# ScalarE instead of SyncE issues the transfers that bring the turned squares of attention back

## The chip, the cores and the metric

The kernel runs on one core of one Trainium2 chip. The metric is device time in microseconds (us), from a single launch; lower is better. The engines of the core are TensorE (PE in the profile), VectorE (DVE), ScalarE (ACT), GpSimd (POOL) and SyncE (SP); each runs its own instructions in the order in which they are written, and a wait in front of an instruction holds back all that is behind it on that engine. DMA transfers are issued by SP, ACT or POOL and moved by 16 DMA engines.

## The reference

```python
x = hidden_states                       # (2, 1024, 512) float32
xn = layernorm(x)
q = dequant_matmul(xn, qw_q, scales_q)  # 32 heads of 128; weights (512, 4096), 4-bit values as int32
k = dequant_matmul(xn, qw_k, scales_k)  # 8 key heads of 128
v = dequant_matmul(xn, qw_v, scales_v)
q, k = apply_rope(q), apply_rope(k)
scores = q @ k.T / sqrt(128)            # causal mask, 1024 x 1024 for each of 2 x 32 heads
ctx = softmax(scores) @ v
attn = dequant_matmul(ctx, qw_o, scales_o)
ffn = xn @ W_base.T + b_base + lora_of_top_2_of_8_experts(xn)
out = x + attn + ffn                    # (2, 1024, 512)
```

A dequantised weight is (value - 8) times a scale that holds for 128 rows of the input dimension.

## The kernel before

All products are made in float32 precision from pairs: every operand is split into a high part (rounded to the format that TensorE takes at full rate) and a low part (the remainder), and three matmuls high x high, low x high and high x low make one product. ScalarE makes most high parts with a copy, POOL and VectorE make the low parts by subtraction.

The work is cut into 16 units (2 batches of 8 key heads; `UNITS`), each with 4 query heads. Below, "unit 9, head 1" is counted from zero; "the second head of a unit" is head 1. Batch `PARKED` is normalised first, parked in HBM, and brought back between unit 7 and unit 8: POOL issues the reload of `xnT_high` and `xnT_low` (line 774), SP that of Y.

A query head goes like this. TensorE makes eight rows of tiles of scores (`scores`, line 1451); row i has i + 1 tiles of 128 x 128. VectorE takes the row's maximum (line 1187), ScalarE the exponential (line 945, `exps`). The second product wants the probabilities transposed. For query rows 0 to 3, and for the part right of the first four key tiles in rows 4 to 7, TensorE transposes them (`turn`, line 1462); ScalarE makes `PT_high` from it (`high`, line 871), VectorE `PT_low` (line 1100). The remaining square, query rows 4 to 7 against keys 0 to 511, is transposed without TensorE. VectorE transposes each of its four row blocks in 32 x 32 pieces (`turn_squares`, line 1194). SP sends each block to HBM (`move_out`, line 594, tile `squares`, 256 KB). When all four have landed, four transfers of 256 KB bring them back in the arrangement that finishes the transpose (`move_in`, line 608, tile `moved`), one for each group of 32 partitions. ScalarE makes `moved_high` from `moved` (`moved_tile_high`, line 871), POOL makes `moved_low` (`moved_tile_low`, line 797), in four tiles j = 0 to 3, with two buffers. `values` (line 1317, output `O_ps`) multiplies turned and moved tiles with V: for c = 0 (query rows 0 to 3) the turned tiles 0 to 3; for c = 1 the order of tiles is 0, 4, 5, 1, 6, 2, 7, 3, of which 0 to 3 are the moved ones. So moved tile 0 is the first thing that c = 1 needs.

Between these steps TensorE projects the queries and keys of the heads to come (`project`) and multiplies finished contexts with the output weights (`output`). A projected half of Q or K passes through VectorE (`terms`, lines 1167 to 1172), POOL (`rope_add`, line 804), ScalarE (`rope_high`, line 871, `Q_high` or `K_high`) and POOL again (`rope_low`, line 812, `Q_low`). POOL also dequantises and splits the weights (lines 738, 739, 758, 759), which SP loads (`load_scales`, line 552; `load_raw`, line 560). A buffer's load waits until POOL has read what stood in it.

The order on TensorE is a list `STEPS`, written by hand from patterns for each head. The order on every other engine is derived from it. `begins` gives each step a planned begin with rough lengths, and `behind(STEPS, us, kinds)` gives for each step of a kind the place in the list at which it is due, `us` microseconds after the planned end of that step. Each engine walks through the list and at each place emits what is due there, in the fixed order of the statements in its loop. For SP: row sums out, squares out (due 3.0 after `scores`), squares in (due 7.0 after the head's last row of scores), row sums in, scales, raw weights, outputs. For ScalarE: high parts of turned tiles (due -0.3), reads of the low-rank product, exponentials (2.6 after `scores`), moved tiles, V, rope copies (4.0 after `project`), contexts. `Seen` leaves out a wait that an earlier one of the same engine already implies.

In the written order, SP's four transfers back stand behind the last transfer out and the load of row sums (`R_sb`), and in the second head of even units behind one pair of weight loads as well; other weight loads that are due soon stand behind them.

Of the kernel before, what the change touches and what calls it, by code (L numbers as in the profile page):

```python
# [178 lines left out]
def behind(steps, us, *kinds):  # L179

    at = begins(steps)
    due, n = [[] for _ in at], 0
    for k, s in enumerate(steps):
        if s[0] in kinds:
            while n < len(steps) and at[n] < at[k] + length(s) + us:
                n += 1
            due[n].append(s)
    return due
# [65 lines left out]
def build_program(nc, x, scales_q, scales_k, scales_v, scales_o, qw_q, qw_k, qw_v, qw_o,  # L254
# [5 lines left out]
    STEPS = tensor_order()  # L260
# [26 lines left out]
    with ctx:  # L287
# [24 lines left out]
        moved = sb("moved", [P, 16, MOVED, 32])  # L312
# [175 lines left out]
        def head_of(u, h):  # L488
            return u * REP + h
# [40 lines left out]
        def _(sp):  # L530
# [63 lines left out]
                sp.dma_start(squares[n % 2][i - 4].rearrange("p (b n) -> p b n", b=4),  # L594
                             row_squares(i).rearrange("p (b n) -> p b n", b=4)).then_inc(moved_out[i - 4], 16)

            def move_in(u, h):
                n = head_of(u, h)
                for i in range(4):
                    if seen.new(moved_out[i], 16 * (n + 1)):  # L600
                        sp.wait_ge(moved_out[i], 16 * (n + 1))
                if n:

                    if seen.new(moved_done, 4 * n):
                        sp.wait_ge(moved_done, 4 * n)
                back = squares[n % 2].rearrange("r (a k) (b n) -> b k (r a) n", a=4, b=4)
                for b in range(4):
                    sp.dma_start(moved[32 * b:32 * (b + 1), :, :, :].rearrange("p t j q -> p t (j q)"),  # L608
                                 back[b]).then_inc(moved_in[n % 2], 16)

            def load_x(b, c):
                if b != PARKED:
                    if seen.new(y_put[c], 16):
# [61 lines left out]
            scales_due, raw_due = weights_due(STEPS, -7.0), weights_due(STEPS, -6.0)  # L675
            sums = behind(STEPS, 3.8, "scores")
            divided, sums_there = behind(STEPS, 0.2, "values"), behind(STEPS, 9.8, "scores")
            squares_out, squares_in = behind(STEPS, 3.0, "scores"), behind(STEPS, 7.0, "scores")
            outputs = behind(STEPS, 1.0, "output")
            turned_now, linear = behind(STEPS, 0.8, "turn_x"), behind(STEPS, 0.6, "lora_b")  # L680
            for n in range(len(STEPS) + 1):
                for _, u, h, i in sums[n]:
                    if i % 4 == 3:
                        store_sums(u, h, i // 4)
                for _, u, h, i in squares_out[n]:
                    if i >= 4:
                        move_out(u, h, i)
                for _, u, h, i in squares_in[n]:
                    if i == 7:
                        move_in(u, h)  # L690

                for _, u, h, i in sums_there[n]:
                    if (u, h, i) == (0, 0, 3):
                        load_sums(u, h, 0)
                for _, u, h, c, j in divided[n]:
                    if j == 3 and (u, h, c) != (UNITS - 1, REP - 1, 1):
                        load_sums(*((u, h, 1) if c == 0 else (*divmod(head_of(u, h) + 1, REP), 0)))
                for u, w in scales_due[n]:
                    load_scales(u, w)
                for u, w in raw_due[n]:  # L700
                    load_raw(u, w)
                for _, u, p, t in outputs[n]:
                    if u + 1 == UNITS and p == 1:
                        store_tile(u // NKV, t)
                    elif u % NKV == NKV - 1 and p == 1 and t % 4 == 3:
                        store_y(u // NKV, t // 4)
                        load_parked_y(t // 4)
                for _, b, t in turned_now[n]:
                    if b == PARKED and t % 4 == 3:
                        load_rows(t // 4)  # L710
                        park_xn(t // 4)
                for _, b, t in linear[n]:
                    if b == PARKED and t % 4 == 3:
                        park_y(t // 4)
                        load_x(STARTED[1], t // 4)
                        if t == 3:
                            load_tables()
# [149 lines left out]
        def _(act):  # L867
# [5 lines left out]
            def linear_weights():  # L873
                for name, src in (("ar", ar_t), ("b", b_t), ("base", w_base_t)):
                    n = {"ar": KT * AR, "b": HID, "base": KT * HID}[name]
                    dst = lin_raw[:, RAW[name]:RAW[name] + n]
                    if name != "b":
                        src, dst = src.rearrange("(k p) n -> p k n", p=P), dst.rearrange("p (k n) -> p k n", k=KT)
                    act.dma_start(dst, src).then_inc(lin_loaded[name], 16)
                act.dma_start(bias[:, :], b_base.to_broadcast([P, HID])).then_inc(lin_loaded["bias"], 16)  # L880
# [29 lines left out]
            def high(*step):  # L910
# [6 lines left out]
                dst, _, src = split_of(step)  # L917
                copy(dst, src).then_inc(pt_high, 1)

            moved_order = itertools.count()  # L920

            def moved_tile_high(u, h, j):
# [52 lines left out]
            moved_due = [behind(STEPS, us, "scores") for us in (15.5, 18.1)]  # L975
            multiplied = behind(STEPS, -0.2, "values")
            divided, low_rank = behind(STEPS, 1.2, "values"), behind(STEPS, -0.6, "lora_a")
            linear_weights()
            linear_weight_high("ar")
            root(PARKED, 0, 2)  # L980
            for n in range(len(STEPS) + 1):
                for s in turned_now[n]:
                    high(*s)
                    if s == ("turn_x", PARKED, 1):
                        root(PARKED, 2, 4)
                        linear_weight_high("b")
                    if s == ("turn_x", PARKED, 3):
                        root(PARKED, 4, 6)
                    if s == ("turn_x", PARKED, 5):
                        root(PARKED, 6, 8)  # L990
                    if s[:2] == ("turn_x", PARKED) and 2 <= s[2] < 2 + KT:
                        linear_weight_high("base", s[2] - 2)
                    if s == ("turn_hidden", PARKED, 1):
                        root(STARTED[1], 0, 4)
                        root(STARTED[1], 4, 8)
                for _, b, t in low_rank[n]:
                    lora_read(b, t)
                    if t == NT - 1:
                        route_exps(b)
                for _, u, h, i in scored[n]:  # L1000
                    exps(u, h, i)
                for j, due in enumerate(moved_due):
                    for _, u, h, i in due[n]:
                        if i == 7:
                            moved_tile_high(u, h, j)
                for _, u, h, c, j in multiplied[n]:
                    if c and j < 2:
                        moved_tile_high(u, h, j + 2)
                for _, u, t in projected[n]:
                    value_high(u, t)  # L1010
                for _, u, w, c in rotated[n]:
                    rope_high(u, w, c)
                for _, u, h, c, j in divided[n]:
                    if j == 3:
                        context_high(u, h, c)
# [566 lines left out]
```

## Time and profile before

| | us |
|---|---|
| median of 2 runs | 2031.91 (2031.89 to 2031.93) |
| the profiled execution, its own time | 2028.99 |
| its span, first to last instruction | 2027.2 |
| TensorE busy | 1987.2 (98%) |
| VectorE busy | 1488.9 (73%) |
| ScalarE busy | 983.2 (48%) |
| POOL busy | 1527.7 (75%) |
| mean granted TensorE clock | 0.996 |
| mean rate of the DMA engines | 138 GB/s |

Busy times are sums of the durations of an engine's instructions; issuing DMAs and waiting are not counted as busy. In the profile, an entry such as `Q_high<-rope` names output and input tile. "idle before <-releaser" is the time an engine stood still ahead of an instruction and what ended it. SPq and ACTq are the sequencers of SP and ACT, where the issue of a transfer is recorded; its duration there is the time that the issue takes on that engine and not the transfer's.

### The profile page before, as it was taken

Reading aid. Unit: us, or ns where it says so; the run is one execution under the profiler, and the core shown is the slowest. Engines: PE = TensorE matmul, PEld = TensorE weight load, DVE = VectorE, ACT = ScalarE, POOL = GpSimd, SP = SyncE. Lnnn points to the kernel's source line nnn. Section 1 sums busy time; section 2 is a strip of 40 time slices with the busy share of each in tenths; the row PEclk is TensorE's granted clock in tenths of the full one; section 3 lists DMA queues with packets and bytes.
Section 4 is the critical chain, followed back from the end, with each engine's and each line's share of the span. In section 5 each row is a group of like instructions: output and inputs, shape, how many; then the busy total and the mean of one; then the engine's idle time right before and its main releaser. Section 6 shows DMA issues by size and latency. Waiting matters only on the chain.

```text
span 2027.2 us, 31353 instructions
## 1 busy us (share of the span) xinstructions
PE 1987.2 (98%) x10666; PEld 1693.1 (84%) x10668; DVE 1488.9 (73%) x3059; ACT 983.2 (48%) x2202; POOL 1527.7 (75%) x1376
## 2 busy tenths in 40 slices
PE   8999999999999999999989999999999999999998
PEld 6888888888888888888878888888888888888887
DVE  6757777777777777677766777777777777767775
ACT  3145554454544455455534545445554545545453
POOL 2657789677878779786886869867787877968683
PEclk9999999999999999999999999999999999999999
DMA  6326465454635546453583645454464545535454
GB/s 227 137 73 154 110 153 136 127 135 120 167 110 136 130 135 158 110 151 105 151 223 110 208 126 157 116 153 128 118 156 115 146 115 155 158 94 141 126 147 112
DMA packets 302422, 280.17 MB, mean 138 GB/s; under 512 B 34584, under 2 KB 215736, under 8 KB 301752
## 3 DMA queue, kind: packets, MB, share of 16 engines
q1 hardware_dynamic: 298808, 272.13, 50.3%
q0 software_dynamic: 2112, 4.19, 0.7%
q8 instruction: 85, 1.39, 0.3%
q10 hardware_dynamic: 1344, 1.85, 0.3%
q14 instruction: 73, 0.60, 0.1%
HBM read 200.25 MB, written 77.94 MB: 137 GB/s over the span
## 4 chain that ended last, share of the span: by engine, by line
PE 74%; DMA 8%; DVE 7%; POOL 7%; issue 2%; SPq 1%; ACT 1%; DVEq 0%; POOLq 0%; ACTq 0%
PE ring L1317 37%; PE O_ps L1317 16%; PE ring L1451 16%; PE turned L1462 5%; DMA moved<-squares 5%; POOL moved_low L797 3%; DMA squares<-probs 2%; DVE probs L1194 2%; DVE ctx_f L1224 1%; POOL scl L739 1%; DVE probs L1187 1%; SPq L608 1%; POOL W_low L759 1%; POOL ctx_low L821 1%; DVE rope L1171 1%
## 5 line engine op out<-in xcount | busy, mean ns | idle before, releaser
L945 ACT ACTIVATE probs<-probs,negmax 128x128 f32<-128x128 f32 (+7 forms) x512 | 396.2, 774 | 153.5 <-DVE negmax L1187 153.3
L1187 DVE CUSTOM_DVE_ANT_0 probs<-ring,mask_row 128x128 f32<-128x128 f32 (+7 forms) x512 | 373.6, 745 | 41.1 <-PE ring L1451 40.8
L797 POOL TENSOR_TENSOR moved_low<-moved,moved_high 128x512 fp32r<-128x512 f32 x256 | 328.7, 1293 | 76.0 <-ACT moved_high L871 74.6
L1100 DVE TENSOR_TENSOR PT_low<-turned,PT_high 128x512 fp32r<-128x512 f32 (+3 forms) x515 | 245.2, 489 | 178.4 <-ACT PT_high L871 97.2
L871 ACT ACTIVATE PT_high<-turned 128x512 fp32r<-128x512 f32 (+3 forms) x515 | 213.6, 433 | 324.1 <-PE turned L1462 301.5
L821 POOL TENSOR_TENSOR ctx_low<-ctx_f,ctx_high 128x512 fp32r<-128x512 f32 (+1 forms) x131 | 165.9, 1267 | 178.2 <-ACT ctx_high L871 178.2
L804 POOL TENSOR_TENSOR rope<-rope 128x512 f32<-128x512 f32 x160 | 206.9, 1293 | 80.9 <-DVE rope L1172 80.9
L1317 PE MATMUL ring<-xnT_high,W_high 128*128 128x512 f32 x640 | 254.9, 398 | 0.0
L1317 PE MATMUL ring<-xnT_high,W_low 128*128 128x512 f32 x640 | 250.6, 392 | 0.0
L1317 PE MATMUL ring<-xnT_low,W_high 128*128 128x512 f32 x640 | 249.5, 390 | 0.0
L1451 PE MATMUL ring<-K_high,Q_high 128*128 128x512 f32 (+3 forms) x768 | 233.9, 359 | 0.9 <-POOL Q_low L812 0.6
L1451 PE MATMUL ring<-K_high,Q_low 128*128 128x512 f32 (+3 forms) x768 | 225.4, 348 | 0.0
L1451 PE MATMUL ring<-K_low,Q_high 128*128 128x512 f32 (+3 forms) x768 | 225.1, 347 | 0.0
L1234 DVE TENSOR_TENSOR Y<-ring,Y 128x512 f32<-128x512 f32 x256 | 175.7, 688 | 62.7 <-PE ring L1317 60.5
L1462 PE MATMUL turned<-ident,probs 128*128 128x128 f32 x1280 | 219.3, 275 | 0.0
L759 POOL TENSOR_TENSOR W_low<-scl,W_high 128x512 fp32r<-128x512 f32 x160 | 206.9, 1293 | 13.3
L739 POOL TENSOR_TENSOR scl<-raw,scl 128x512 f32<-128x512 f32 x160 | 206.7, 1292 | 13.4
L1167 DVE TENSOR_TENSOR rope<-ring,cos_sb 128x512 f32<-128x512 f32 x160 | 110.7, 692 | 143.2 <-PE ring L1317 137.9
L871 ACT ACTIVATE moved_high<-moved 128x512 fp32r<-128x512 f32 x256 | 159.5, 626 | 112.0 <-DMA moved<-squares 59.9
L871 ACT ACTIVATE Q_high<-rope 128x512 fp32r<-128x512 f32 x128 | 80.9, 632 | 267.3 <-POOL rope L804 267.3
L1317 PE MATMUL ring<-W_high,ctx_high 128*128 128x512 f32 x512 | 206.9, 404 | 1.4 <-POOL ctx_low L821 1.4
L1317 PE MATMUL ring<-W_high,ctx_low 128*128 128x512 f32 x512 | 201.2, 393 | 0.0
(124 smaller groups left out, 4680.6 us busy)
## 6 DMA issues: line engine op xcount, KB each, us to landing
squares<-probs SPq DMA_DIRECT2D x256, 256.0 KB, 2.9
moved<-squares SPq DMA_DIRECT2D x256, 256.0 KB, 4.7
R_sb<-row_sums SPq DMA_DIRECT2D x128, 256.0 KB, 3.7
scl<-packed_q SPq DMA_DIRECT2D x64, 256.0 KB, 5.0
raw<-in_qw_q SPq DMA_DIRECT2D x64, 256.0 KB, 5.0
scl<-in_scales_o SPq DMA_DIRECT2D x64, 256.0 KB, 4.7
raw<-in_qw_o SPq DMA_DIRECT2D x64, 256.0 KB, 2.9
scl<-packed_k SPq DMA_DIRECT2D x16, 256.0 KB, 4.2
```

Source lines behind the costliest of these rows:

```text
L739: nc.gpsimd.tensor_tensor(out=scl[:, n % 2, :], in0=as_float, in1=scl[:, n % 2, :], op=ALU.mult).then_inc(scaled, 1)
L759: nc.gpsimd.tensor_tensor(out=W_low[:, slot, :], in0=scl[:, n % 2, :], in1=W_high[:, slot, :].bitcast(f32), op=ALU.subtract).then_inc(w_do ...
L797: nc.gpsimd.tensor_tensor(out=low, in0=moved[:, :, j, :], in1=high.bitcast(f32), op=ALU.subtract).then_inc(moved_done, 1)
L804: nc.gpsimd.tensor_tensor(out=rope_a[:, n % 2, :], in0=rope_a[:, n % 2, :], in1=rope_b, op=ALU.add).then_inc(rope_sum, 1)
L821: nc.gpsimd.tensor_tensor(out=ctx_low[:, at, cols], in0=ctx_f[:, cols], in1=ctx_high[:, at, cols].bitcast(f32), op=ALU.subtract).then_inc( ...
L871: return nc.scalar.activation(dst, src, ACT.Copy)
L945: nc.scalar.activation(probs[:, at], probs[:, at], ACT.Exp, bias=negmax[:, i:i + 1], scale=-1.0, accum_out=sums[:, i:i + 1]).then_inc(exp_ ...
L1100: nc.vector.tensor_tensor(out=dst, in0=src, in1=high.bitcast(f32), op=ALU.subtract).then_inc(pt_low, 1)
L1187: nc.vector.tensor_tensor_reduce(row, ps, hidden_keys, -1.0, -MASKED, ALU.add, ALU.min, negmax[:, i:i + 1]).then_inc(negmax_ready, 1)
L1317: mm = nc.tensor.matmul(dst, lhs, rhs, start=start and n == 0, stop=stop and n == len(terms) - 1)
L1451: mm = nc.tensor.matmul(ps[:, lo:hi], lhs[:, tile], moving, start=first, stop=last)
L1462: mm = nc.tensor.transpose(turned_place(step)[:, q * P:(q + 1) * P], probs[:, at:at + P], ident[:, :])
```

## The change

`move_in` is taken out of SP's program and put into ScalarE's, with the same waits (all four blocks landed in HBM; the moved tiles of the head before read by POOL), the same four transfers and the same semaphores. It keeps its due time, 7.0 us after the last row of scores. In ScalarE's loop it stands behind the exponentials and ahead of the moved tiles.

```diff
@@ SP @@
-            def move_in(u, h):
-                n = head_of(u, h)
-                for i in range(4):
-                    if seen.new(moved_out[i], 16 * (n + 1)):
-                        sp.wait_ge(moved_out[i], 16 * (n + 1))
-                if n:
-
-                    if seen.new(moved_done, 4 * n):
-                        sp.wait_ge(moved_done, 4 * n)
-                back = squares[n % 2].rearrange("r (a k) (b n) -> b k (r a) n", a=4, b=4)
-                for b in range(4):
-                    sp.dma_start(moved[32 * b:32 * (b + 1), :, :, :].rearrange("p t j q -> p t (j q)"),
-                                 back[b]).then_inc(moved_in[n % 2], 16)
...
-            squares_out, squares_in = behind(STEPS, 3.0, "scores"), behind(STEPS, 7.0, "scores")
+            squares_out = behind(STEPS, 3.0, "scores")
...
-                for _, u, h, i in squares_in[n]:
-                    if i == 7:
-                        move_in(u, h)
@@ ScalarE @@
+            def move_in(u, h):
+                n = head_of(u, h)
+                for i in range(4):
+                    if seen.new(moved_out[i], 16 * (n + 1)):
+                        act.wait_ge(moved_out[i], 16 * (n + 1))
+                if n:
+
+                    if seen.new(moved_done, 4 * n):
+                        act.wait_ge(moved_done, 4 * n)
+                back = squares[n % 2].rearrange("r (a k) (b n) -> b k (r a) n", a=4, b=4)
+                for b in range(4):
+                    act.dma_start(moved[32 * b:32 * (b + 1), :, :, :].rearrange("p t j q -> p t (j q)"),
+                                 back[b]).then_inc(moved_in[n % 2], 16)
...
+            squares_in = behind(STEPS, 7.0, "scores")
...
                 for _, u, h, i in scored[n]:
                     exps(u, h, i)
+                for _, u, h, i in squares_in[n]:
+                    if i == 7:
+                        move_in(u, h)
                 for j, due in enumerate(moved_due):
```

## Rows read from the trace of the kernel before

**Rows 1.** Waits of TensorE: engine, line, waited for, us in total, times, longest.
```profile
PE O_ps L1317 <- POOL moved_low L797: 9.1, 8, 6.4
```

**Rows 2.** Waits of SP's sequencer, the same columns.
```profile
SPq L601 <- DMA squares<-probs: 160.1, 64, 4.7
```

**Rows 3.** Chain of waits from 1010 to 1045 us: start, us, what.
```profile
1016.69 3.81 DMA squares<-probs
...
1020.65 0.32 SPq L608
...
1022.60 12.06 DMA moved<-squares
```

**Rows 4.** Timeline of SP, unit 9, head 1: start, us, instruction, count.
```profile
1238.04 1.91 SPq L608 DMA_DIRECT2D moved<-squares  x4
...
1240.86 0.43 SPq L560 DMA_DIRECT2D raw<-in_qw_q  x1
```

**Rows 5.** Timeline of ScalarE, the same head.
```profile
1236.18 0.98 ACT L871 ACTIVATE PT_high<-turned 128x512 fp32r<-128x512 f32 x2 [2.55 <-PE turned L1462]
1237.89 0.63 ACT L871 ACTIVATE Q_high<-rope 128x512 fp32r<-128x512 f32 x1 [0.73 <-POOL rope L804]
1239.50 0.38 ACT L871 ACTIVATE PT_high<-turned 128x256 fp32r<-128x256 f32 x1 [0.98 <-PE turned L1462]
```

**Rows 6.** Timeline of POOL, the same head.
```profile
1239.89 1.29 POOL L812 TENSOR_TENSOR Q_low<-rope,Q_high 128x512 fp32r<-128x512 f32 x1
...
1245.13 1.29 POOL L812 TENSOR_TENSOR Q_low<-rope,Q_high 128x512 fp32r<-128x512 f32 x1 [0.74 <-ACT Q_high L871]
1246.38 2.55 POOL L797 TENSOR_TENSOR moved_low<-moved,moved_high 128x512 fp32r<-128x512 f32 x2
```

**Rows 7.** Timeline of TensorE, the same head.
```profile
1243.39 0.28 PE L1317 MATMUL O_ps<-PT_high,V_high 128*128 128x256 f32 x1
...
1248.35 0.39 PE L1317 MATMUL O_ps<-moved_high,V_high 128*128 128x512 f32 x1
```

**Rows 8.** Timeline of SP, unit 1, head 2.
```profile
308.43 2.90 SPq L608 DMA_DIRECT2D moved<-squares  x4
```

**Rows 9.** Timeline of POOL, the same head.
```profile
309.90 1.30 POOL L812 TENSOR_TENSOR Q_low<-rope,Q_high 128x512 fp32r<-128x512 f32 x1
...
316.38 2.71 POOL L797 TENSOR_TENSOR moved_low<-moved,moved_high 128x512 fp32r<-128x512 f32 x2
```

**Rows 10.** Timeline of TensorE, the same head.
```profile
318.35 0.39 PE L1317 MATMUL O_ps<-moved_high,V_high 128*128 128x512 f32 x1
```

**Rows 11.** The tile moved: its issues, with duration in ns min/median/max.
```profile
L608 SPq DMA_DIRECT2D moved<-squares x256: 303/487/1820, 135.5 to 2002.8; - x128
```

**Rows 12.** Timeline of ScalarE's sequencer at the start, two of its four issues.
```profile
0.75 0.46 ACTq L879 DMA_DIRECT2D probs<-in_ar_t  x1
...
2.27 0.85 ACTq L880 DMA_DIRECT2D R_sb<-in_b_base  x1
```

**Rows 13.** DMA queues from 1026 to 1029 us: packets, MB, share of 16 engines.
```profile
q0 software_dynamic: 376, 0.77, 84.3%
q1 hardware_dynamic: 368, 0.18, 43.5%
```

**Rows 14.** Chain of waits of the whole span, one of its longest pieces.
```profile
282.01 7.23 DMA moved<-squares
```

**Rows 15.** Timeline of ScalarE, unit 2, head 1.
```profile
413.18 0.63 ACT L871 ACTIVATE moved_high<-moved 128x512 fp32r<-128x512 f32 x1 [2.94 <-DMA moved<-squares]
```

**Rows 16.** Timeline of TensorE, the same head.
```profile
415.24 0.49 PE L1317 MATMUL O_ps<-moved_high,V_high 128*128 128x512 f32 x1
```

**Rows 17.** Busy time by stretch: PE, PEld, DVE, ACT, POOL, PEclk, DMA share, GB/s.
```profile
1036.00:1040.00 4.00, 3.30 (x9) 2.62 (x9) 2.06 (x7) 2.98 (x9) 3.45 (x4) 0.50 1.24 382
1040.00:1044.00 4.00, 4.00 (x20) 3.50 (x18) 2.46 (x9) 2.57 (x7) 3.92 (x5) 0.76 0.56 156
```

**Rows 18.** Page, part 3, a DMA queue: packets, MB, share of 16 engines.
```profile
q10 hardware_dynamic: 1344, 1.85, 0.3%
```

## The prediction

> **What bounds the kernel now.** I read the waits of TensorE first, because the page gives it 98% of the span. The reader is to see how little of its idle time hangs on the moved tiles: 9.1 us in 8 waits, and 6.4 us of that is one wait [rows 1]. Even a perfect change cannot return more than that and the clock time behind it; the rest of 2027 us is TensorE at work. Next SP's own waits: 64 waits at line 601, 160.1 us, released by a DMA and not by an engine, 2.5 us each [rows 2]. So when SP comes to the moved square it is early and waits for the last square to reach HBM. The chain shows one case whole: the last square is issued at 1016.69 and lands 3.81 us later, at 1020.50, and SP issues the first transfer back at 1020.65, 0.15 us after it [rows 3]. I compared the two times in all 64 heads; the distance is 0.09 to 0.16 us in every one. **SP is never late**, so ScalarE cannot issue earlier; it issues at the same moment, or later if it is busy. Then I read ScalarE, POOL and TensorE in that stretch of a head, in a head of unit 9 [rows 4 to 7] and one of unit 1 [rows 8 to 10].
>
> **What is moved: one wait and four issues a head.** Taken off SP: the wait (2.5 us) and four issues of 0.49 us median, together 1.91 us in the unit 9 head and 2.90 us in the unit 1 head [rows 4, 8]; the longest single issue took 1.82 us [rows 11]. What SP holds behind them are the loads of the next weight's scales and raw values and later of the row sums. POOL needs those loads many microseconds later, so SP's freedom is worth nothing by itself: 0. If POOL did wait for them, the cover would be TensorE's own queue of ready work.
>
> Put on ScalarE: its position. Working out the written order gives, for the second and third heads of a unit, PT_high of turned tiles 0 and 1, then the four issues, then the first Q_high, then PT_high of tiles 2 and 3. Price of one issue on ScalarE: the trace has only its four loads at the start, the first 0.46 and the longest 0.85 us [rows 12]; SP's median for the transfers in question is 0.49 [rows 11], near the first. The same four transfers are issued, so I take SP's own durations head by head (about 1.95 us for four) and keep 4 x 0.85 = 3.4 us as the upper end, 4 x 0.30 = 1.2 us (SP's shortest) as the lower.
>
> *Turned tiles behind the issues.* In unit 9, ScalarE is free at 1237.16 (two copies from 1236.18, 0.98 us) [rows 5]. It would wait for the landing, issue from 1238.04 to 1239.95, do Q_high until 1240.63 and the next PT_high until 1241.0, where it now starts at 1239.50. TensorE takes that tile at 1243.39 [rows 7], and only VectorE's short subtraction lies between. Cover 2.4 us, so 0. If it were gone each microsecond of ScalarE would be one of TensorE.
>
> *Q_high, and POOL behind it.* This is what is late next. Q_high moves from 1237.89 to 1240.00, ends at 1240.63, and Q_low on POOL starts at 1240.70 and not at 1239.89: +0.8 us [rows 5, 6]. From that Q_low to moved_low POOL has no free time but 0.74 us [rows 6], and that is its own round trip to ScalarE for the second half, which moves along. So moved_low starts at 1247.2 and not at 1246.38; the first of the pair (half of 2.55 us, 1.27) ends at 1248.45. TensorE now reads it at 1248.35 [rows 7]. Stall: 0.1 us. In unit 1: issues 308.43 to 311.33, Q_high to 312.0, Q_low at 312.05 for 309.90, +2.15 us; moved_low, now 316.38 to 317.67, ends at 319.8; TensorE reads at 318.35 [rows 8 to 10]. Stall: 1.45 us. I did the same for every head. 20 get a stall, nearly all in the first three heads of odd units: 0.03 to 1.9 us each, together 12 us. With 1.2 us for four issues the same working gives 2 us, with 3.4 us it gives 45.
>
> *The other heads.* In the fourth heads and the first heads of even units the copy behind the issues slips by up to 4 us too, but TensorE reads the moved tile 4 to 6 us after it is ready: 0. The third heads of even units have 1.2 us and slip by nothing. In the last head nothing but turned tile 4 is behind the issues and it starts after them: 0.
>
> *The transfers.* SP's raw load now starts while the moved square is in flight, on another queue; before it stood behind it. I price the overlap by the reload between batches, where two queues were busy: 376 packets of one, 368 of the other, one for one [rows 13]. A 256 KB load beside a 1024 KB square that takes 7.2 us from its last issue to landing [rows 14] can cost up to a quarter of its flow, 1.3 us, and 0 if it falls outside. It counts only where nothing else covers it, as in the second heads of even units: there moved_high starts as the data lands (idle 2.94 us until the DMA) and TensorE reads the product at once [rows 15, 16]. About ten such heads at 0.3 us: 3 us (0 to 13). The Trainium skill says in "DMA: Bandwidth & Descriptors", section "Issuing engines are not separate DMA queues", that DMAs of all issuers run on the same 16 engines and interleave, so that another issuer saves sequencer time alone. By that rule the sum has no gain; the packets of rows 13 agree.
>
> *The change of batch.* The 6.4 us wait is the moved square of unit 7, head 2, 12.06 us in flight [rows 1, 3] beside the xnT reload; the granted clock is 0.50 from 1036 to 1040 right after TensorE stood still [rows 17], the 1.2 GHz level. ScalarE would issue at the same 1020.6; a third queue makes it a little later: +1 us (-9 to +6).
>
> **Sum.** 12 + 3 + 1 = +16 us on the profiled execution, which took 2028.99 us with a span of 2027.2. The median of the runs is 2031.91, 2.9 us above it; I add the 16 to that: **2048 us**.
>
> **Rivals.**
> 1. *All of it is hidden.* POOL's chain or TensorE's waits shift as a whole and the small stalls take each other's place: 2032, between 2028 and 2036. For it: 44 of 64 heads get no stall in the working above, and 16 of the 20 others under 1 us. Against: POOL's gapless stretch [rows 6].
> 2. *ScalarE becomes the bound, slower by over 2%.* Place: Q_high behind the four issues. Price: if an issue on ScalarE costs what the longest seen there did, 0.85 us, the POOL step above gives 45 us and not 12, and with transfers and reload 49: 2081. With SP's longest, 1.82 us, the same working stalls 55 heads for 207 us: 2243. It passes 2% (41 us in all) from about 0.8 us an issue. For it: both engines now issue at once, and the unit 1 head shows 2.90 us for four where 1.91 is usual [rows 4, 8]. Against: the 0.85 us transfer repeats one row over all partitions, the squares don't.
> 3. *A gain at the change of batch.* The square, alone on its queue, is served sooner; the 6.4 us wait goes, and so does the half clock behind it (half of 3.3 us and 0.24 of 4 us [rows 17], 2.6 us): 2032 - 9 = 2023. Against: the reload takes half of the packets in either case.
> 4. *The issuer is moved but nothing else*, since the queues are one: then rows of ScalarE's queue would be missing. The page has a queue of 1.85 MB, which is the sum of ScalarE's four loads [rows 18], so it has one of its own. I give this no chance of its own; its time would be that of rival 1.
>
> **Chances.** Forecast (4 to 38 us slower) 0.60; rival 1 0.22; rival 3 0.07; rival 2 0.11, of which 0.10 over 2%. A difference of 2% is about what a measurement of this kernel can tell from no change. The range takes in rival 1 and the forecast: 2028 to 2070. So over 2% faster 0.01, within 2% 0.89, over 2% slower 0.10.
>
> **What would show it.** ScalarE's queue has 256 issues of about 0.5 us (near 0.85: rival 2). The first starts 0.1 to 0.2 us after the last square lands. Q_high and Q_low in the unit 9 head start about 2.1 and 0.8 us later against TensorE's own work. TensorE's waits for moved_low grow from 8 to some 25 and from 9.1 to about 25 us, each under 2 us, with no half clock. SP issues raw before the fourth moved transfer. If TensorE's waits for moved_low stay at 9 us, the POOL step is wrong; if they shift to PT_low, the cover of turned tiles is.

## The result: 2109.31 us, 3.9% slower

The changed kernel takes 2109.31 us (two runs, 2105.49 and 2113.14) against 2031.91, a ratio of 1.0391 with a 95% interval of 1.0364 to 1.0418. The forecast was 2048 with a range to 2070: the sign was right, the size was not (+77 us measured, +16 forecast). The profiled execution has a span of 2111.3 us against 2027.2.

**The profile after.** First the page of the changed kernel: busy time by engine, the two hardware DMA queues (packets, MB, share of 16 engines), and the issues of the tile that was moved (KB each, median us to landing).

```profile
PE 2011.9 (95%) x10668; PEld 1700.0 (81%) x10668; DVE 1486.6 (70%) x3059; ACT 970.7 (46%) x2202; POOL 1530.2 (72%) x1376
...
q1 hardware_dynamic: 163640, 205.01, 33.1%
q10 hardware_dynamic: 136512, 68.98, 16.5%
...
moved<-squares ACTq DMA_DIRECT2D x256, 256.0 KB, 5.7
```

ScalarE's queue, q10, had 1.85 MB [rows 18] and has 68.98 now: the change does what it says. The span outside PE's busy time was 2027.2 - 1987.2 = 40.0 us and is 2111.3 - 2011.9 = 99.4: 59 of the 84 us are TensorE standing still. PE's busy time grew by 24.7 us for the same matmuls, and the mean granted clock of the execution (view of cores) fell from 0.996 to 0.986. That is at most 21 us, an estimate (0.014 x 2111 less 0.004 x 2027): in part of the time at the lower clock TensorE stands still anyway. Experiment 2 has what else makes busy time grow. The bytes to be moved are the same, but the tile takes 5.7 us to land where it took 4.7.

TensorE's waits, in the view of waits (us in total, times, longest):

```profile
PE O_ps L1318 <- POOL moved_low L780: 51.4, 30, 15.2
PE O_ps L1318 <- DVE PT_low L1101: 18.9, 21, 2.6
```

The first answers to [rows 1], 9.1 us in 8 waits: +42.3. Sorted by head, the first heads of odd units have 20.6 us of it (1.3 before), the head at the change of batch 15.2 (6.4), and the other second and third heads of odd units 10.9 (0.8). The wait for PT_low was this in the kernel before, the same view:

```profile
PE O_ps L1317 <- DVE PT_low L1100: 4.4, 6, 1.9
```

It grew by 14.5. Together 57 of the 59 us. The issues themselves and the time to landing, from the view of the tile moved:

```profile
L914 ACTq DMA_DIRECT2D moved<-squares x256: 309/510/1395, 134.5 to 2086.9; - x128
...
DMA to landing us min/median/max: 3.0/5.8/21.9
```

An issue on ScalarE costs 0.51 us where SP's cost 0.49 [rows 11]: ScalarE is hardly the dearer engine.

**The head of rows 4 to 7**, unit 9, head 1, in the changed kernel. SP, ScalarE, POOL and TensorE, one timeline each:

```profile
1291.87 0.43 SPq L552 DMA_DIRECT2D scl<-packed_q  x1
1296.53 0.38 SPq L560 DMA_DIRECT2D raw<-in_qw_q  x1
```

```profile
1292.75 0.98 ACT L854 ACTIVATE PT_high<-turned 128x512 fp32r<-128x512 f32 x2 [2.54 <-PE turned L1463]
1295.28 1.93 ACTq L914 DMA_DIRECT2D moved<-squares  x4
1297.25 0.63 ACT L854 ACTIVATE Q_high<-rope 128x512 fp32r<-128x512 f32 x1 [3.52 <-issue]
1297.79 0.54 ACT L854 ACTIVATE PT_high<-turned 128x256 fp32r<-128x256 f32 x2
```

```profile
1297.96 1.29 POOL L795 TENSOR_TENSOR Q_low<-rope,Q_high 128x512 fp32r<-128x512 f32 x1 [1.46 <-ACT Q_high L854]
...
1303.21 1.30 POOL L795 TENSOR_TENSOR Q_low<-rope,Q_high 128x512 fp32r<-128x512 f32 x1 [0.74 <-ACT Q_high L854]
1304.47 2.52 POOL L780 TENSOR_TENSOR moved_low<-moved,moved_high 128x512 fp32r<-128x512 f32 x2
```

```profile
1305.80 0.50 PE L1318 MATMUL O_ps<-moved_high,V_high 128*128 128x512 f32 x1 [0.72 <-POOL moved_low L780]
```

This is the step that the forecast described: the copies of [rows 5] wait behind 1.93 us of issues, Q_low behind Q_high, moved_low behind that, and TensorE waits 0.72 us where 0.1 us was forecast. The forecast left the issues where SP had them. They start 0.7 us later, measured from the start of the PT_high ahead of them (2.53 us behind it, 1.86 in [rows 4, 5]), because the last square lands later. In experiment 2 they start 1.0 us later in this head and the wait is 0.99 us, so the slip needs no change of the loads. In [rows 8 to 10]'s head, unit 1, head 2, the forecast was a stall of 1.45 us; TensorE's timeline there:

```profile
332.13 0.50 PE L1318 MATMUL O_ps<-moved_high,V_high 128*128 128x512 f32 x1 [1.30 <-POOL moved_low L780]
```

**What the forecast did not have** is in the first head of the same unit 9. Changed kernel, timelines of SP, then ScalarE, then TensorE:

```profile
1262.21 0.46 SPq L552 DMA_DIRECT2D scl<-packed_q  x1
1264.10 0.38 SPq L560 DMA_DIRECT2D raw<-in_qw_q  x1
```

```profile
1264.40 2.07 ACTq L914 DMA_DIRECT2D moved<-squares  x4
...
1274.84 0.63 ACT L854 ACTIVATE moved_high<-moved 128x512 fp32r<-128x512 f32 x1 [2.44 <-DMA moved<-squares]
```

```profile
1276.86 0.49 PE L1318 MATMUL O_ps<-moved_high,V_high 128*128 128x512 f32 x1 [2.08 <-POOL moved_low L780]
```

SP, free of the wait, issues the scales 2.2 us before the squares and the raw load 0.3 us before them. In the kernel before, SP did it the other way round, in the same head:

```profile
1211.50 1.91 SPq L608 DMA_DIRECT2D moved<-squares  x4
1213.45 0.49 SPq L552 DMA_DIRECT2D scl<-packed_q  x1
1213.98 0.43 SPq L560 DMA_DIRECT2D raw<-in_qw_q  x1
```

The DMA queues in the changed kernel, from 0.4 us before the first issue of the squares (1264 to 1267 us) and then from 1267 to 1270 us (packets, MB, share of 16 engines):

```profile
q1 hardware_dynamic: 403, 0.47, 84.3%
q10 hardware_dynamic: 10, 0.01, 0.6%
```

```profile
q10 hardware_dynamic: 939, 0.47, 76.4%
q1 hardware_dynamic: 349, 0.19, 30.4%
```

and in the kernel before in the 3 us from its first issue, 1211.5 to 1214.5:

```profile
q1 hardware_dynamic: 971, 0.57, 73.2%
```

In the 2.6 us from its first issue the square gets 10 packets through; before, the one queue moved 971 in 3 us, most of them the square's (819 if the window starts 0.4 us earlier, as above). It lands 10.4 us after the first issue (1274.8); before, `moved_high` started without waiting, at most 7.0 us after the first issue:

```profile
1218.46 0.62 ACT L871 ACTIVATE moved_high<-moved 128x512 fp32r<-128x512 f32 x1
```

Over the eight first heads of odd units the mean from first issue to landing went from 7.3 to 10.7 us, over the third heads of even units it stayed at 7.0. Over the third heads of odd units it went from 7.9 to 10.1, much of that at the change of batch (14.0 to 23.3); the other seven went from 7.1 to 8.2. Behind the 2.08 us wait of unit 9, head 0, TensorE's granted clock is 0.50, the 1.2 GHz level; the columns are those of [rows 17]:

```profile
1278.00:1280.00 2.00, 2.00 (x8) 1.61 (x6) 1.11 (x6) 1.03 (x4) 1.83 (x3) 0.50 0.00 0
```

**The change of batch**, unit 7, head 2. From the chain of waits, and by stretch (the columns of [rows 17]):

```profile
1060.30 21.88 DMA moved<-squares
```

```profile
1084.00:1088.00 4.00, 3.78 (x9) 3.02 (x10) 2.40 (x8) 2.51 (x8) 3.57 (x5) 0.50 0.00 0
```

The piece of [rows 3] that was 12.06 us is 21.88; TensorE stands 15.2 us where it stood 6.4, and works on at the 1.2 GHz level (0.50) behind it, as in [rows 17].

### The profile page after: what moved, and what is told of

The parts are those of the page before. It is cut to its first block, busy times and chain, and to the rows that moved or that the text cites. A ratio compares the mean times of both kernels' runs of the same rounds, so it can differ in the third digit from the quotient of the medians.

```text
span 2111.3 us, 31355 instructions
## 1 busy us (share of the span) xinstructions
PE 2011.9 (95%) x10668; PEld 1700.0 (81%) x10668; DVE 1486.6 (70%) x3059; ACT 970.7 (46%) x2202; POOL 1530.2 (72%) x1376
## 3 DMA queue, kind: packets, MB, share of 16 engines
q10 hardware_dynamic: 136512, 68.98, 16.5%
## 4 chain that ended last, share of the span: by engine, by line
PE 49%; DMA 16%; POOL 13%; DVE 10%; issue 4%; ACTq 3%; ACT 3%; SPq 1%; DVEq 0%; POOLq 0%
PE ring L1318 21%; PE O_ps L1318 13%; PE ring L1452 12%; DMA moved<-squares 9%; DMA squares<-probs 6%; POOL moved_low L780 4%; DVE probs L1195 3%; ACTq L914 3%; PE turned L1463 3%; POOL rope L787 2%; DVE probs L1188 2%; POOL W_low L742 2%; POOL Q_low L795 2%; POOL scl L722 1%; DVE ctx_f L1225 1%
## 5 line engine op out<-in xcount | busy, mean ns | idle before, releaser
L854 ACT ACTIVATE PT_high<-turned 128x512 fp32r<-128x512 f32 (+3 forms) x515 | 207.9, 431 | 230.5 <-PE turned L1463 209.0
L795 POOL TENSOR_TENSOR Q_low<-rope,Q_high 128x512 fp32r<-128x512 f32 x128 | 165.5, 1293 | 98.1 <-ACT Q_high L854 98.0
```

The costliest lines, as they stand in the source:

```text
L795: nc.gpsimd.tensor_tensor(out=low[:, half(c)], in0=rope_a[:, n % 2, :], in1=high[:, half(c)].bitcast(f32), op=ALU.subtract).then_inc(rope_ ...
L854: return nc.scalar.activation(dst, src, ACT.Copy)
```

## The experiments

Two theories. **A, the order of the loads**: SP, no longer held by the wait, sends its loads ahead of the squares, and the squares land late. **B, the block**: what was forecast, the issues standing ahead of Q_high on ScalarE, but costing more than 12 us. Each kernel's ratio is to the kernel before on the same chip; a point is 1% of its time, about 20 us.

**1. SP held back again.** Changed kernel; SP waits at its old place, for ScalarE's first copy behind the issues (e1_gate_issued), or until the squares have landed (e1_gate_landed).

```diff
+                for _, u, h, i in squares_back[n]:
+                    copies = sum(len(x) for x in ropes[:n]) + 1
+                    if i == 7 and copies <= len(rope_number) and seen.new(rope_high_done, copies):
+                        sp.wait_ge(rope_high_done, copies)
```

> The changed kernel, but SP waits, at the place where it used to issue the squares back, for ScalarE's first rope copy behind the four issues, so that SP's loads of scales and raw weights go out only after the squares, as before. Theory A (order of transfers: SP's freed loads get ahead of the squares and lengthen their flight from about 7 to 10 or 11 us in the first heads of odd units): flight back to about 7 us, and time back to 2035 to 2050. Theory B (ScalarE's four issues hold back Q_high and with it POOL's chain): the issues still stand there, so 2095 to 2110.

> The same, but SP waits until all four squares have landed, so that no weight load overlaps them at all. Theory A: flight 7 us or less everywhere, 2035 to 2050, unless the weight loads, now 7 us later, come too late for POOL (then its waits for raw grow). Theory B: 2095 to 2110.

Measured: 2059.09 us, 1.0156 (1.0118 to 1.0194), and 2060.49, 1.0161 (1.0135 to 1.0188). Both lie between the two forecasts, so neither theory is the whole. The queues of e1_gate_issued in unit 9, head 0, in the 3 us from 0.4 us before its first issue (1233.71 to 1236.71):

```profile
q10 hardware_dynamic: 746, 0.37, 45.3%
q1 hardware_dynamic: 68, 0.11, 10.4%
```

The square has the engines again (746 packets for 10), median to landing 4.6 us, and 2.3 of the 3.9 points are gone, about 48 us. That is A. The rest of 1.6% is not.

The two kernels differ in one place that tells of the second queue. TensorE's waits for moved tiles in the one and in the other:

```profile
PE O_ps L1323 <- POOL moved_low L785: 30.1, 26, 12.8
```

```profile
PE O_ps L1322 <- POOL moved_low L784: 24.0, 23, 6.4
```

The longest is at the change of batch. In e1_gate_issued SP's scales go out there 3.9 us after the first issue of the squares, behind all four, as in the kernel before (3.8 us), and POOL's reload begins 0.6 and 1.1 us ahead. The main difference left is the queue (and with it the raw load, which goes out 4.3 us after the first issue and not 6.2). The square is 20.9 us on its way, before 14.0; with SP held until the landing it is 14.7. So beside the reload the loads on a second queue delay the squares, even when they are issued behind them. Elsewhere the median to landing shows nothing of the kind.

**2. The block alone.** Kernel before; `stand_in` is called on ScalarE where the change calls `move_in`, does the same waits and issues four transfers of 2 KB each. SP still brings the squares back.

```diff
+            def stand_in(u, h):
+                n = head_of(u, h)
+                for i in range(4):
+                    act.wait_ge(moved_out[i], 16 * (n + 1))
...
+                for b in range(4):
+                    act.dma_start(dump[4 * n + b], ident[32 * b:32 * b + 32, 0:16]).then_inc(dumped, 16)
```

> The kernel before, in which SP still issues the squares back; ScalarE has in addition, where the changed kernel puts them, the same waits and four small transfers (2 KB each, to a place in HBM that nobody reads). It has ScalarE's block without any change of SP's order. Theory A: only my working of POOL's chain, +5 to +15 us, 2037 to 2047. Theory B: most of the loss, 2090 to 2110.

Measured: 2054.13 us, 1.0126 (1.0098 to 1.0155). TensorE's waits there:

```profile
PE O_ps L1335 <- POOL moved_low L799: 20.9, 23, 5.6
...
PE O_ps L1335 <- DVE PT_low L1118: 7.5, 11, 1.3
```

The wait for moved tiles grew by 11.8 us in 15 more waits: the forecast's "12" to the microsecond. That it is so close is luck: in unit 9, head 1, the wait is 0.99 us for a forecast of 0.1. And the time grew by 26, which again lies between the two forecasts. In the profiled execution, 28.7 us longer, TensorE stands 12.5 us more (52.5 for 40.0) and is busy 16.2 us more (2003.4 for 1987.2). Of the latter some 7 us are not the block's: they come from a stretch at the 1.2 GHz level before the first square goes back, from 23 to 44 us, 20.5 us long where the kernel before has 6.8. The other three runs, at a mean clock of 0.995 to 0.996 like the kernel before (0.991 to 0.998), are 24 to 29 us slower all the same.

The remaining 9 us fit what a stop costs beyond its wait. In a row of matmuls the next starts 0.23 us after the last, though each is recorded with 0.39; the changed kernel, unit 9, head 0:

```profile
1277.19 0.39 PE L1318 MATMUL O_ps<-moved_low,V_high 128*128 128x512 f32 x1
1277.42 0.40 PE L1318 MATMUL O_ps<-moved_high,V_low 128*128 128x512 f32 x1
```

A stop loses that overlap of 0.16 us, and the first matmul behind it takes 0.49 us, 0.1 more: up to 0.27 us that no wait shows, an estimate. The weight loads (PEld) of this product stop for `moved` 38 times more; the view of the tile, in the kernel before and in this one:

```profile
  PEld O_ps L1317: 16.6, 24
```

```profile
  PEld O_ps L1335: 39.9, 62
```

38 such stops are up to 10 us. e1_gate_landed agrees: 63 stops, busy time up by 9.9 us at the same mean clock of 0.996. This share is worked out and not tested. Theory A is absent here: 4.8 us to landing.

**3. The waits without issues, and the issues behind the rope copy.** As 2, without the four transfers (e8_wait_only); as 2, with waits and transfers due 8.2 us instead of 7.0 and behind `rope_high` in ScalarE's order (e11_block_behind).

```diff
-            stand_ins = behind(STEPS, 7.0, "scores")
+            stand_ins = behind(STEPS, 8.2, "scores")
```

> The kernel before, with ScalarE standing in the waits for the four moved squares at the place where the change puts them, and issuing nothing: SP still issues the transfers. It splits the +25.8 us that the same waits with four small transfers cost (2054.13 against 2026.87). Theory (the chain Q_high on ScalarE, Q_low and moved_low on POOL, then the turned tiles behind it): ScalarE is released at the landing, 0.2 us before SP's first issue, and has no 2 us of issues. By the same head-by-head working as the forecast, with 0 for the issues, 0 to 3 us of stalls: 1.000 to 1.003 of before. Rival (the waits themselves cost, since ScalarE can not run its copies before the landing): 15 us or more, ratio 1.007 or above, and TensorE's waits for PT_low stay near the 7.5 us of the kernel with small transfers.

> The kernel with the waits and the four small transfers on ScalarE (2054.13 us, 1.0126 of before) with the same waits and transfers moved one place down in ScalarE's order: behind the rope copy Q_high or K_high of that moment. Theory (POOL waits for that copy): Q_low starts at its old time, the stalls on moved_low (20.9 us in 23 waits there) go back to about 10, while the turned tiles behind the issues stay as late or get later; 1.002 to 1.007 of before. Rival (it is ScalarE's whole queue that is late, the turned tiles above all, or the small transfers disturb the large ones): no less than 1.011, with PT_low waits above 7.5 us.

Measured: 2026.54 us, 0.9995 (0.9978 to 1.0011), and 2028.7, 1.0002 (0.9986 to 1.0019). TensorE's wait for moved tiles in the one and in the other:

```profile
PE O_ps L1332 <- POOL moved_low L799: 7.8, 7, 5.4
```

```profile
PE O_ps L1335 <- POOL moved_low L799: 9.5, 10, 7.1
```

Both are at [rows 1]'s level. Waiting on ScalarE costs nothing; four issues cost 1.3% ahead of Q_high and nothing one copy further down and 1.2 us later. The second came out below what was expected of it: the turned tiles behind the issues (PT_low 5.3 us in 5 waits) were covered after all. B is shown, and its place with it.

**4. Is it the second queue, or the order?** Kernel before, SP's loads due 4 us earlier, so that they go out ahead of the squares on the *same* queue.

```diff
-            scales_due, raw_due = weights_due(STEPS, -7.0), weights_due(STEPS, -6.0)
+            scales_due, raw_due = weights_due(STEPS, -11.0), weights_due(STEPS, -10.0)
```

> The kernel before with one edit: SP's loads of scales and raw weights are due 4 us earlier, so that in many heads they stand ahead of the squares back on SP's own queue; ScalarE is not touched. Theory A: flight 9 to 11 us or a later issue in the first three heads of odd units, 2050 to 2100. Theory B: nothing on ScalarE changed, 2030 to 2035.

Measured: 2109.44 us, 1.0403 (1.0375 to 1.0430). SP in unit 9, head 0:

```profile
1259.17 0.45 SPq L552 DMA_DIRECT2D scl<-packed_q  x1
1261.37 0.38 SPq L560 DMA_DIRECT2D raw<-in_qw_q  x1
1261.92 3.95 SPq L608 DMA_DIRECT2D moved<-squares  x4
```

The order of the changed kernel, made on one queue, with a loss as large: the order does its harm without a second queue. The size is not A's alone. Four issues here take 3.95 us for 1.91, and in the second heads of odd units SP, busy with its loads, starts them 1.2 us after the last square has landed (mean; 0.15 before), neither of which the changed kernel has. So this kernel bounds A and does not measure it; it came out above its expected range.

**5. Which load?** Changed kernel; the scales of q and k, one 2 KB row repeated over all 128 partitions, read 128 different rows of another input (e5_scales_rows), or the raw values of q and k read whole 2 KB rows and not 512 B pieces (e6_raw_rows). Both compute other values for q and k. The first line is of the one, the second of the other.

```diff
+                    src = w_base_t[0:P, :].rearrange("p (k n) -> p k n", k=KT)
...
+                    dst, src = raw[:, :], qw_o[n % 32 * P:(n % 32 + 1) * P, :]
```

> The changed kernel; the scales of q and k weights are loaded from 128 different rows of another matrix (2 KB each, contiguous) and not from one 2 KB row repeated to all partitions, so the output is another. Same bytes and packets. If the repeated row is what holds up the squares (its packets take 0.22 to 0.30 us where others take 0.1), flight in the first heads of odd units falls from 10.7 to about 8.5 us and the time to 2070 to 2090. If it is the number of packets or bytes ahead, nothing changes: 2100 to 2112.

> The changed kernel; the raw values of q and k weights are loaded from 128 contiguous rows of 2 KB of another matrix and not as 512 pieces of 512 B, so the output is another. Same bytes, a quarter of the packets. If the 512 B packets of raw, one for one with the squares' 512 B packets, hold them up: flight in the first heads of odd units falls to about 9 us, time 2070 to 2090. If the scales do it: 2100 to 2112.

Measured: 2094.5 us, 1.0291 (1.0259 to 1.0323), and 2109.07, 1.0373 (1.0342 to 1.0404). The queues of e5_scales_rows in unit 9, head 0, in the 3 us from 0.4 us before its first issue:

```profile
q1 hardware_dynamic: 664, 0.55, 58.8%
q10 hardware_dynamic: 403, 0.20, 22.8%
```

The squares get 403 packets where they got 10, with the same bytes asked for. From first issue to landing the first heads of odd units take 8.5 us, as expected, though the time lies a little above the expected range; with other raw rows they take 10.8. So the repeated row is a part of A, about 1 point (between two chips; the source also lies in another tensor, which was not separated); the shape of the raw load shows no effect outside the intervals. Landing stays slow in other heads (median 5.5 us), so the scales are not all of A; how the rest divides between raw values, scales and row sums stays open.

**6. The change of batch.** Kernel before with the xnT reload, due 1.2 us after the last projections of unit 7, due 14 us (e4_reload) or 7.5 us (e9_reload_mid) after them; e7_reload_later is e4 with SP's loads due 2 us later (-5 and -4 for -7 and -6); e10_reload_after is the changed kernel with 7.5.

```diff
+            parked_back = behind(STEPS, 7.5, "project")
...
-                    if u == PARKED * NKV - 1 and w == "q3":
-                        load_parked_xn(c)
+                for _, u, w, c in parked_back[n]:
+                    if u == PARKED * NKV - 1 and w == "q3":
+                        load_parked_xn(c)
```

> The kernel before; POOL issues the reload of xnT between the batches later (due 14 us after the last projections of unit 7 and not 1.2), behind the flight of that head's squares. SP and ScalarE are untouched. If the reload is what stretches that flight to 14 us: the 6.4 us wait and the half clock behind it go, about 9 us faster, 2015 to 2020 against 2027. If the flight stays, no change.

> The same with one edit more: SP's loads of scales and raw weights are due 2 us later, so that they no longer stand ahead of the squares in the second heads of even units (flight there 8.6 us). If loads ahead of the squares cost time, 1 to 4 us faster than with the later reload alone; if they become late for POOL, slower.

> The kernel before with the reload of xnT at the change of batch due 7.5 us after the last projections of unit 7, where it is 1.2 us there. With 14 us the 6.4 us wait for the moved square went and a 4.4 us wait for xnT came in the next head, and the time stayed (2036.4, 1.0003). Theory (both are one wait for the same DMA engines, and there is a place where neither is waited for): 5 to 9 us less, ratio 0.9955 to 0.998. Rival (the square and the reload need together more transfer time than that stretch has): one of the two waits is there again, in parts, and the ratio is 0.999 to 1.001.

> The changed kernel with the same move of the reload (7.5 us instead of 1.2). Its longest wait for a moved tile is 15.2 us, in head 2 of unit 7, where its square is 23.3 us on its way, with half clock behind it. Theory (the change of batch is a part of its own, about 12 to 20 us of the 77): 2085 to 2097 us, ratio 1.026 to 1.032, with that wait under 5 us. Rival (the square is late there for the scales and raw loads and not for the reload): wait and time stay, 2105 to 2112.

Measured: e4 2036.4 us, 1.0003 (0.9987 to 1.0019), not the 9 us faster that were expected. The 6.4 us wait is gone and this one is there instead:

```profile
PE ring L1319 <- DMA xnT_low<-xn_parked: 4.4, 1, 4.4
```

e9, between the two places: 2021.08 us, 0.9964 (0.9950 to 0.9978), with neither wait. Its moved tiles:

```profile
PE O_ps L1319 <- POOL moved_low L797: 4.7, 10, 1.1
```

This is the **fastest kernel of the study**: 0.4%, small, but its interval excludes no change. e10: 2092.29, 1.0317 (1.0286 to 1.0348), the longest wait 3.6 us for 15.2. That is 0.74 points under the change; 0.36 of them the same edit gives the kernel before. That leaves about 0.4 points, 8 us, as the change's own damage at the change of batch, but the intervals of the ratios together are as wide; what bears it out is the wait, 15.2 us for 6.4. e7 came out at 2124.79, 1.0439 (1.0405 to 1.0472). POOL's waits there:

```profile
POOL raw L738 <- DMA raw<-in_qw_q: 83.8, 29, 6.8
```

Loads due 2 us later throughout starve POOL (11.5 us in 4 waits for this tile in the kernel before); 4 us earlier (experiment 4) they starve the squares. The gap is not narrow everywhere: e1_gate_landed sends the loads that stand behind the squares about 5 us later than the kernel before (in unit 9, head 0, 6.8 us after the first issue for 2.0) and loses nothing by it against e1_gate_issued.

**7. Do A and B make up the whole?** Changed kernel with B removed (e12_behind: `move_in` due 8.2, behind `rope_high`), with A and B removed (e13_behind_gated: also SP waits until the squares have landed, due 8.2), and with the reload at 7.5 besides (e14_both_reload).

```diff
-            squares_in = behind(STEPS, 7.0, "scores")
+            squares_in = behind(STEPS, 8.2, "scores")
```

> The changed kernel with only the place of ScalarE's wait and issues moved: behind the rope copy (Q_high or K_high) of that moment, where they stand ahead of it now. If the two causes add (issues ahead of Q_high, about 1.3%, and SP's loads getting ahead of the squares, about 2.5%), the first goes and the second stays: ratio 1.022 to 1.032, with first heads of odd units still about 10 us on their way from the first issue to the landing. Rival (both are one cause, the late Q_high, and the slow transfers only follow from it): under 1.015.

> The changed kernel with both causes removed: ScalarE issues behind the rope copy, and SP waits at the old place of its issues, due 8.2 instead of 7.0 us, until the squares have landed. Theory (nothing else is in the 3.9%): ratio 1.001 to 1.009; not 1.000, since the squares start up to 0.7 us later, behind a copy, and TensorE waits for the transfers in about 10 heads. Rival (a third cause, such as ScalarE's queue being slower than SP's, or the turned tiles behind the issues): 1.012 or more.

> The same with the reload of xnT due 7.5 us after the last projections of unit 7, as in the kernel that came out at 0.9964 of before. Theory (the change of batch is a matter of its own, and adds): 3 to 9 us under the kernel beside it, 0.997 to 1.005 of before. Rival (the later squares need the time that the later reload freed): no less than the kernel beside it.

Measured: 2082.35 us, 1.0266 (1.0235 to 1.0297); 2045.33, 1.0080 (1.0049 to 1.0112); 2041.55, 1.0070 (1.0046 to 1.0094). The first two lie where the two separate causes put them. Time to landing in the first and in the second:

```profile
DMA to landing us min/median/max: 3.0/5.3/21.5
```

```profile
DMA to landing us min/median/max: 3.0/4.7/12.5
```

| ratio to before | SP free | SP held back |
|---|---|---|
| issues ahead of Q_high | 1.0391 | 1.0161 |
| issues behind it | 1.0266 | 1.0080 |

The upper right value is e1_gate_landed's. B is worth 1.3 points with SP free and 0.8 with SP held; A 2.3 with the issues ahead of Q_high and 1.9 with them behind. All but 0.8 points (16 us) of the loss goes with the two. What is left may be the price of mending B in this way: in half of the heads the issues start on the mean 0.9 to 1.4 us after the last square has landed, behind the copy (0.2 in the changed kernel). That is argued from the trace and not tested, and a share of the second queue is not ruled out. e14 lies 0.1 points under e13, inside both intervals: not told apart, where 3 to 9 us were expected.

## Why the forecast was wrong, step by step

- *"SP is never late"*, ScalarE issues at the same moment: right. The issues start 0.17 us after the last square lands in the median, 0.21 at most.
- *Price of an issue*: right, 0.51 us.
- *Q_high, and POOL behind it, 12 us*: the path is right, and the sum of waits (11.8 us in experiment 2). Single heads are less so: 1.45 forecast and 1.30 measured in unit 1, but 0.1 forecast and 0.99 in unit 9 (0.72 in the changed kernel); the closeness of the sum is partly luck. As time it was mis-sized: 26 us in experiment 2, with 3.1 us of PT_low and some 9 us that each stop costs beyond its wait.
- *Turned tiles behind the issues, 0, and "the other heads", 0*: wrong. PT_low went from 4.4 to 18.9 us in the changed kernel. In the fourth heads of odd units turned tile 1 stands behind the issues and the rope copy, and TensorE waits 0.2 to 1.2 us for it, 3.4 us in all; experiment 2, with the issues alone, has these waits too. A larger part, 7.3 us for 0.6, are waits in the fourth heads of even units some 20 us after the issues. They are missing in experiment 2 (0.6 us) and in e1_gate_issued (0.9) and present where the loads were moved (4.7 in experiment 4), so they go with the loads; their path was not traced.
- *"SP's freedom is worth nothing by itself: 0"*: **the step that failed.** I asked only who waits for SP's loads, and nobody does. I did not ask what the loads do when they leave 2 us sooner. They take the DMA engines just as the squares start: about 48 us of the 77 go when SP is held back (experiment 1).
- *The transfers, 3 us (0 to 13)*: the same mistake as a price. It rested on an even exchange of packets [rows 13], on the raw load alone, and on its 256 KB; the scales, issued first, were left out, and the squares got 10 packets of 413. The working was loose as well: a quarter of the 7.2 us is 1.8 us, not 1.3. The rule drawn from "DMA: Bandwidth & Descriptors" (Trainium skill, "Issuing engines are not separate DMA queues"), that another issuer saves sequencer time alone, held as far as there was no gain. It says nothing of what a freed sequencer sends next, and that is where the time went here.
- *The change of batch, +1 (-9 to +6)*: wrong in size, 15.2 us of wait for 6.4; about +8 in time. The "third queue" of the forecast is a real part of it: with the old order and the second queue the wait is 12.8 us (experiment 1).
- *"With no half clock"*: wrong. In the profiled execution ten stretches are at the 1.2 GHz level, 61 us together, for four and 18 us before. Five of them are at waits of 2.1 to 3.6 us in first heads of odd units, where the forecast had each wait under 2 us. Half of the difference is the 21 us that the clock can have cost at most.

Of the rivals, 1 and 3 are ruled out by the interval and 4 by the 68.98 MB of ScalarE's queue. Rival 2 named one of the right places (Q_high behind the issues) with a price that did not occur: 0.51 us an issue, not 0.85. Its 2081 was nearer for the wrong reason. To anything over 2% slower the forecast had given a chance of 0.10.

## What to carry to other kernels

When a wait is taken off an issuing engine, list what it held back, and ask of each transfer what it will collide with; a wait can be the only thing that keeps a background load from passing one that is urgent. When issues are put on a computing engine, it is their place among its copies that counts: 2 us ahead of the head of POOL's chain cost 1.3%, one copy further down and 1.2 us later nothing. Price a stall in time and not in waits alone: here 11.8 us more of waiting came with 26 us more of time.

## What the runs showed of the hardware that I had not expected

- A load that repeats one 2 KB row over 128 partitions can hold the DMA engines far longer than its bytes say: in the 3 us window of unit 9, head 0, the 2 KB packets of SP's queue took 0.15 us in the median and over 0.3 us for a tenth of them, and the squares got 10 packets; with 128 different rows 0.08 us, and the squares got 403.
- An issue costs nearly the same for 2 KB as for 256 KB: median 0.46 us for the four small transfers of experiment 2, 0.51 for the squares.
- Two queues did not always share one for one: 403 packets to 10 in that window, 664 to 403 with a like lead of SP's queue but different rows, and 368 to 376 in [rows 13].
- Transfers issued behind others on one queue and on a second one are not the same: at the change of batch the squares took 14.0 us with the loads behind them on their own queue, 20.9 us with the loads issued behind them on the other (experiment 1).
